# Keeping a convolution block's scan inputs and gate in PSUM, in place: scans of 512 columns, VectorE's stages split at their links, 28 places for expert states, new orders

## What is computed

```
x = x + L0_conv(ln(x)) ; x = x + L0_ffn(ln(x)) ; x = x + L1_conv(ln(x)) ; x = x + L1_ffn(ln(x))

conv:  inp, og, fg = split(z @ in_w + in_b, 3)
       inp, og, lam = silu(inp), sigmoid(og), sigmoid(fg)
       inp_f = (1 - lam)[..., d, None] * inp[..., None, e]        # per head 2 x 2, so 128 channels
       h_t = lam_t * h_{t-1} + inp_f_t     along rows and along columns, forward and reverse, summed
       out = sum_d state[..., d, e] * og[..., d];  layernorm * gamma + beta;  @ out_w + out_b
L0_ffn: 16 experts of 128, top 2 of softmax;  silu(z @ w1) * (z @ w2) @ w3, weighted
L1_ffn: 8 experts of 256, top 2;              gelu(z @ W1 + b1) @ W2 + b2, weighted
```

## Time and profile before

| | us |
|---|---|
| median of three runs (261.26 to 262.43) | 261.69 |
| the profiled execution | 262.96 |
| its span, first to last instruction | 261.1 |
| busy: PE / DVE / ACT / POOL | 217.1 / 219.8 / 166.8 / 162.6 |
| mean granted TensorE clock | 0.961 |

### The profile page before, as it was taken

One profiled execution on the slowest core, in us unless ns is written; L12 is line 12 of the kernel. 1 busy time (PEld: TensorE's weight loads), 2 busy tenths in 40 slices (PEclk: granted clock), 3 DMA queues, 4 the chain that ended last, 5 costly groups with the idle time before them and its releaser, 6 DMA issues.

```text
span 261.1 us, 3879 instructions
## 1 busy us (share of the span) xinstructions
PE 217.1 (83%) x1013; PEld 134.5 (52%) x1013; DVE 219.8 (84%) x591; ACT 166.8 (64%) x392; POOL 162.6 (62%) x182
## 2 busy tenths in 40 slices
PE   0843887698999797999799888779698998989992
PEld 0633854477676545665355446246445636465441
DVE  3988899999999899999999999999986979517033
ACT  3572887279447375546486547789679986684570
POOL 3565589658558642776738989657657787704232
PEclk9999999599799997799999999999799999999999
DMA  3790015855205900049100950000520070052621
GB/s 113 156 227 12 1 33 134 171 87 127 38 1 115 203 13 0 0 105 204 21 0 7 216 107 1 1 0 0 124 43 0 4 161 3 1 120 47 144 57 40
DMA packets 20210, 18.52 MB, mean 71 GB/s; under 512 B 5703, under 2 KB 15069, under 8 KB 20189
## 3 DMA queue, kind: packets, MB, share of 16 engines
q1 hardware_dynamic: 20168, 18.28, 33.9%
q10 hardware_dynamic: 20, 0.00, 0.0%
HBM read 17.56 MB, written 0.72 MB: 70 GB/s over the span
## 4 chain that ended last, share of the span: by engine, by line
PE 36%; DVE 31%; issue 14%; POOL 10%; ACT 7%; DMA 1%; POOLq 1%; DVEq 0%; ACTq 0%
PE bank L1059 12%; PE bank L1060 10%; PE bank L1166 8%; POOL total L619 5%; DVE hidden L1005 5%; PE bank L1063 4%; DVE weighted L1024 3%; DVE rev_h L942 2%; ACT hidden L782 2%; ACT norm_e L661 2%; DVE rows L967 1%; DVE rev_w L942 1%; DVE shift_a L893 1%; DVE fwd_h L941 1%; DVE best_at L990 1%
## 5 line engine op out<-in xcount | busy, mean ns | idle before, releaser
L1059 PE MATMUL bank<-tok_z,up_hi 128*128 128x512 f32 (+1 forms) x224 | 91.3, 414 | 6.6 <-DVE rows L967 1.4
L1060 PE MATMUL bank<-tok_z,up_lo 128*128 128x512 f32 (+1 forms) x224 | 84.4, 381 | 0.0
L619 POOL TENSOR_TENSOR total<-total,weighted 128x512 f32<-128x512 f32 (+1 forms) x47 | 58.5, 1245 | 22.0 <-DVE weighted L1027 12.3
L1166 PE MATMUL bank<-hidden,down 128*64 128x512 f32 (+1 forms) x288 | 64.2, 571 | 3.1 <-DVE hidden L1005 2.0
L1059 PEld LDWEIGHTS bank<-tok_z,up_hi 128*128 128x128 f32 x224 | 45.7, 204 | 31.1 <-issue 12.7
L773 ACT ACTIVATE silu_h<-bank 128x512 f32<-128x512 f32 (+1 forms) x80 | 40.2, 513 | 25.4 <-PE bank L1060 19.2
L1060 PEld LDWEIGHTS bank<-tok_z,up_lo 128*128 128x128 f32 x224 | 46.0, 205 | 5.4
L782 ACT ACTIVATE hidden<-bank,expert_bias 128x512 f32<-128x512 f32 x64 | 40.5, 689 | 8.6 <-PE bank L1060 8.4
L1005 DVE TENSOR_TENSOR hidden<-silu_h,bank 128x512 f32<-128x512 f32 (+1 forms) x80 | 42.8, 567 | 0.5 <-PE bank L1060 0.5
L1166 PEld LDWEIGHTS bank<-hidden,down 128*64 128x64 f32 x288 | 18.3, 141 | 36.1 <-issue 22.1
L1024 DVE TENSOR_TENSOR weighted<-bank,gates_b 128x512 f32<-128x512 f32 (+1 forms) x35 | 19.6, 574 | 0.4 <-POOL total L619 0.4
(11 more groups left out here) (126 smaller groups left out, 392.6 us busy)
## 6 DMA issues: line engine op xcount, KB each, us to landing
gates_b<-gates_dram SPq DMA_DIRECT2D x12, 512.0 KB, 6.3
gates_b<-gates_dram SPq DMA_DIRECT2D x6, 1024.0 KB, 9.8
up_raw<-in_L_ffn_w_dram SPq DMA_DIRECT2D x8, 192.0 KB, 4.5
up_raw<-in_L_ffn_W_dram SPq DMA_DIRECT2D x2, 512.0 KB, 6.3
up_raw<-in_L_ffn_w_dram SPq DMA_DIRECT2D x4, 128.0 KB, 2.8
down<-in_L_ffn_w_dram SPq DMA_DIRECT2D x1, 512.0 KB, 7.6
down<-in_L_ffn_W_dram SPq DMA_DIRECT2D x1, 512.0 KB, 7.8
out_dram<-rows SPq DMA_DIRECT2D x4, 128.0 KB, 4.1
```

Of the source, the lines that this page charges most:

```text
L619: nc.gpsimd.tensor_tensor(t, t, weighted[:, n % WEIGHTED, 0:c], ALU.add).then_inc(s_sum, 1)
L1059: nc.tensor.matmul(dst, hi, z, start=True, stop=False)
L1060: return nc.tensor.matmul(dst, lo, z, start=False, stop=True)
L1166: last = nc.tensor.matmul(t[k * D:(k + 1) * D, 0:c], w, hidden_of(first + k, j), start=(j == 0), stop=(j == l))
```

## The change

The scan inputs stay in PSUM. `vi` writes the silu back to bank `I`, where it came from; `aw` makes the row scans' input there in place, and `ca` writes the turned copy into bank `F`, which `tf` has read. `to` writes the gate's tanh back to bank `O`. `value_i`, `tanh_o`, `add_w` and `add_h` are gone. So the banks are freed later: `I` and `F` by the column scans (`sc`), `O` by `og`. In PE's string `vi`, `tf` and `to` are no longer names that free a bank.

With no padding a scan is over 512 columns, and the factor that cuts a sequence off is a zero in the factors: forward scans have it at a sequence's first position, reverse scans at its last, hence two sets of factors in each direction, `lam_fw`, `lam_rw`, `lam_fh`, `lam_rh`, of 15 out of 16 columns each, written by two ACT instructions in place of one. Both scan stages wait for `ca` (before, `sw` waited for `aw` alone).

DVE's functions are cut at their links into stages with names of their own (`a0 a1 a2`, `e0 e1 e2`, `lh lg ma pl mk`, `xh x`, `av aw`), so that other work can stand between. `NORM_BY_SCALAR` shrinks: the rows of units 5 to 8 are normalised by DVE. `HIDDENS` goes from 16 to 28, `WEIGHTED` from 2 to 3. All strings are new; SP's loads of layer 1's `in` and `down` weights come before the first gates. `BY_POOL` is empty, so the paths for it add no instruction.

```diff
-NORM_BY_SCALAR = {"a": (2, 3, 4, 5, 6, 7, 8), "e": (2, 3, 4, 5, 6, 7, 8)}
-SILUS, HIDDENS, WEIGHTED = 3, 16, 2
+NORM_BY_SCALAR = {"a": (2, 3, 4), "e": (2, 3, 4)}
+SILUS, HIDDENS, WEIGHTED, COPIES = 3, 28, 3, 2
...
 SP_ORDER = """
-gates up1 in1 gates gates gates gates gates gates gates gates store store store store
+in1 gates up1 gates gates gates gates gates gates gates gates store store store store
...
-        FREED = {"za": s_z["a"], "ze": s_z["e"], "tf": s_tanh_f, "vi": s_value, "to": s_tanh_o, "y": s_conv,
+        FREED = {"za": s_z["a"], "ze": s_z["e"], "sc": s_scan_h, "og": s_gated, "y": s_conv,
...
             def pads(_):
-                for t in (lam_w, lam_h, add_w, add_h):
-                    last = nc.gpsimd.memset(t[:, 0:SCAN:PAD], 0.0)
+                for t in (lam_fw, lam_fh):
+                    nc.gpsimd.memset(t[:, 0:TOK:SEQ], 0.0)
+                for t in (lam_rw, lam_rh):
+                    last = nc.gpsimd.memset(t[:, SEQ - 1:TOK:SEQ], 0.0)
...
             def value(u):
+                t = bank("I", u)[:, 0:c]
...
+                if u in ONE_SILU:
+                    nc.scalar.activation(t, t, ACT.Silu, bias=column(l, I_B)).then_inc(s_value, 1)
+                    return
...
+                nc.scalar.activation(tanh_i[:, 0:c], t, ACT.Tanh, bias=half_bias[:, I_B, l:l + 1], scale=0.5)
+                nc.scalar.activation(t, t, ACT.Identity, bias=column(l, I_B)).then_inc(s_value, 1)
...
+            def lambdas(t, u, n, ap):
+                return nc.scalar.activation(square(t, u)[:, :, :, n], ap[:, :, :, n], ACT.Copy, bias=0.5, scale=0.5)
...
-                nc.scalar.activation(by_image(body(lam_w, u), u), square(tanh_f, u), ACT.Copy, bias=0.5,
-                                     scale=0.5).then_inc(s_lam_w, 1)
+                lambdas(lam_fw, u, slice(1, SEQ), square(tanh_f, u))
+                lambdas(lam_rw, u, slice(0, SEQ - 1), square(tanh_f, u)).then_inc(s_lam_w, 1)
...
+                t = bank("O", u)[:, 0:c]
+                nc.scalar.activation(t, t, ACT.Tanh, bias=half_bias[:, O_B, l:l + 1], scale=0.5).then_inc(s_tanh_o, 1)
...
-                nc.scalar.activation(turned(body(add_h, u), u), by_image(body(add_w, u), u),
-                                     ACT.Copy).then_inc(s_add_h, 1)
+                nc.scalar.activation(turned(bank("F", u), u), square(bank("I", u), u), ACT.Copy).then_inc(s_add_h, 1)
...
+                lambdas(lam_fh, u, slice(1, SEQ), turned(tanh_f, u))
+                lambdas(lam_rh, u, slice(0, SEQ - 1), turned(tanh_f, u)).then_inc(s_lam_h, 1)
...
-                nc.vector.scalar_tensor_tensor(by_image(body(add_w, u), u), square(tanh_f, u), 1.0, square(value_i, u),
-                                               ALU.subtract, ALU.mult).then_inc(s_add_w, 1)
+                nc.vector.scalar_tensor_tensor(t, tanh_f[:, 0:c], 1.0, t, ALU.subtract, ALU.mult).then_inc(s_add_w, 1)
...
-                    dve.wait_ge(s_add, u + 1)
+                    c = columns_of(u)
+                    add = bank(src, u)
+                    dve.wait_ge(s_add_h, u + 1)
...
-                    nc.vector.tensor_tensor_scan(fwd[:, 0:end], lam[:, 0:end], add[:, 0:end], 0.0, ALU.mult, ALU.add)
-                    nc.vector.tensor_tensor_scan(rev[:, end:0:-1], lam[:, end:0:-1], add[:, end:0:-1],
+                    nc.vector.tensor_tensor_scan(fwd[:, 0:c], lam_f[:, 0:c], add[:, 0:c], 0.0, ALU.mult, ALU.add)
+                    nc.vector.tensor_tensor_scan(rev[:, c - 1::-1], lam_r[:, c - 1::-1], add[:, c - 1::-1],
                                                  0.0, ALU.mult, ALU.add).then_inc(s_scan, 1)
...
-                nc.vector.scalar_tensor_tensor(gated[:, 0:c], tanh_o[:, 0:c], 1.0, gated[:, 0:c],
+                nc.vector.scalar_tensor_tensor(gated[:, 0:c], bank("O", u)[:, 0:c], 1.0, gated[:, 0:c],
```

More of the change, by code:

```diff
@@ L8 @@
 SEQ = 16
-PAD = SEQ + 1
 IMAGE = H * W
@@ L12 @@
 TOK = 2 * IMAGE
-SCAN = 2 * SEQ * PAD + 1
 MOST = 2 * HALF
@@ L112 @@
 PAIR = [(u, q) for u in range(len(UNITS)) for q in range(EXPERTS[layer(u)] // 2)]
-STEPS_0 = sum(1 for u, _ in STEP if layer(u) == 0)
+STEPS_OF = [[n for n, (u, _) in enumerate(STEP) if layer(u) == l] for l in range(LAYERS)]
 def pairs_before(u):
@@ L150, in residents, with by_pool_before @@
     first, end = images(u)
-    return [v for v in range(SECOND) if images(v)[0] < end and images(v)[1] > first]
+    return [v for v in range(len(UNITS)) if layer(v) == 0 and images(v)[0] < end and images(v)[1] > first]
+def by_pool_before(n):
+    return sum(m < n for m in BY_POOL)
 def chunk(pair):
@@ L507, in store_rows @@
             def store_rows(v):
-                u = SECOND + v
+                u = [u for u in range(count) if layer(u)][v]
                 first, end = images(u)
@@ L514, in _ @@
             played(SP_ORDER, {"in1": second_in, "up1": second_up, "gates": broadcast_gates, "store": store_rows})
-            sp.wait_ge(s_out, 16 * (count - SECOND))
+            sp.wait_ge(s_out, 16 * sum(layer(u) for u in range(count)))
         @block.gpsimd
@@ new lines, in aggregate, with make, spreads @@
+            def aggregate(n):
+                def make(u):
+                    dve.wait_ge(s_stats[n], u + 1)
+                    for k in range(tiles_of(u)):
+                        last = nc.vector.bn_aggr(moments[n][:, k, :], stats[n][:, k, :])
+                    last.then_inc(s_moments[n], 1)
+                return make
+            def spreads(n, eps):
+                def make(u):
+                    t = tiles_of(u)
+                    dve.wait_ge(s_moments[n], u + 1)
+                    if u:
+                        dve.wait_ge(s_rstd[n], u)
+                    nc.vector.tensor_scalar(spread[n][:, 0:t], moments[n][:, 0:t, 1], eps, None,
+                                            ALU.add).then_inc(s_spread[n], 1)
+                return make
@@ L990, in choose, with marks @@
                     last = nc.vector.max_index(best_at[:, k, :], best[:, k, :], logits[:, k, 0:e])
-                link(last)
+                last.then_inc(s_found, 1)
+            def marks(u):
+                e, t = EXPERTS[layer(u)], tiles_of(u)
+                dve.wait_ge(s_found, u + 1)
                 if u:
```

326 lines of the change are left out of this document (175 added, 151 removed).

## The result

The changed kernel takes **243.73 us** (median of 4 runs, 242.28 to 244.6) beside 261.58 for the kernel before in the same rounds: a ratio of 0.9307, with a 95% interval from 0.9257 to 0.9358. That is 17.9 us less. The forecast was 254.5 in a range from 244 to 264: the sign was right, the size was not, and the time lies just under the range. The gain is more than twice the 7.2 us that were forecast.

What follows compares the result with a forecast made beforehand. DVE was taken to bound the kernel, lengthened by waits for POOL. DVE -13.0 (-21.1 + 9.3 - 1.2), banks +2.1 and tail +3.7 gave -7.2 us: 254.5 from a median of 261.69, range 244 to 264.

Steps and rivals of the forecast that it cites:

- What bounds the kernel: From 20 to 200 us DVE, busy 171.5 of 180 us, is what all other engines run behind.
- Scans, row inputs, gate, silu: DVE instructions reading a bank escape the wait for POOL: -12.4, -5.1, -2.7 and -0.9, together -21.1 us.
- the rival in which the bank doesn't end the wait: Wait due to SBUF factors or the output; scans give only 3.0 us: +10.9, 272.6 us; chance 0.04.
- Normalising, +9.3: Units 5 to 8 on DVE: 32 tiles add 15.3 us, eight small products save 6.0; between +4.0 and +14.7.
- Links, -1.2 (0 to -2.5): Work put between dependent DVE steps fills about half of some 2.5 us idle time behind links.
- Banks, +2.1: PE up steps while two or more banks hold a conv product: 45 more, at 0.047 us each.
- The rival that runs out of banks: PE stops for lack of banks held up by DVE's scans: slower, 263 to 270 us; chance 0.13.
- Places and the third buffer, nothing taken: A third `weighted` buffer and 28 places let PE and DVE run further apart; no time counted.
- Tail, +3.7: After the last logits PE has eight pairs of down products, not six; two pairs take 3.65 us.
- three signs of being wrong: Scans slower from a bank, DVE's normalising tiles hanging on POOL, or DVE below 90% busy between 20 and 190 us.
- all goes well, under 250: Normalising tiles at 0.312 us (+4.0), no price for banks, links filled: -15.9, 245.8 us; chance 0.20.
- nothing comes of it: PE waits on the chain through POOL, so DVE's saved 13 us become idle: about 261 us; chance 0.13.

Runs made afterwards that it cites:

- gates by pairs: Changed kernel with the last two units' gates broadcast in one 128 KB transfer per pair and half, not two of 512 KB: 239.44 us, ratio 0.914.

## Why the prediction was wrong

*What bounds the kernel.* Right for the kernel before (6.2 us of time for 7.3 off DVE). **The step that failed** is the one from DVE's time to the kernel's, "nearly each microsecond taken off it moves what follows", carried through to the end of the sum: after the change 12.4 us off DVE bring 1.0. The sum added gains and losses on DVE as if each were worth its duration on either side. Two of its terms show it, normalising and links.

*Scans, row inputs, gate, silu.* Forecast -21.1 on DVE. By the durations of both traces it was -12.0 (51.1 to 39.0), -4.9, -2.6 and -0.9, together -20.4. The mechanism and the prices were right, and the rival in which the bank doesn't end the wait is out. Not in the sum: other instructions with two inputs in SBUF got shorter too, the low parts by 4.2 us (`parts_e` from 0.83 to 0.53), which fits POOL's being busy 20.6 us less.

*Normalising, +9.3.* The largest loss of the sum, and **mis-sized**. 32 tiles added 14.5 us of durations (means of 0.41 and 0.51, within the bounds), and the small products gave back 9.5 where I had 6.0: +5.0 from trace to trace. Undone in the changed kernel it is 11.8 us of DVE's busy time. The price in time was nothing either way (243.4 with ACT, 243.7 with DVE); without it the forecast would have been 245.2.

*Links, -1.2 (0 to -2.5).* Wrong as a step, not only in size: I priced the idle time in front of a waiting step. DVE's busy time fell by 26.7 us, its durations by 20.3; the other 6.4 are overlap between neighbours, which the idle column can't show, and the `hidden` products between the steps keep PE going. Undone, the split costs 13.5 us, where the sum had 1.2.

*Banks, +2.1.* PE's waits for column scans, gate, `hidden` and `weighted` sum to 1.3 + 2.7 + 0.5 + 1.1 = 5.6, under the 7 that I had set as the sign of the forecast. In the kernel before the same waits of its products were 0 + 1.4 + 2.9 + 1.1 = 5.4, so that nearly nothing was added:

```profile
PE bank L1166 <- DVE hidden L1005: 2.0, 2, 1.4
PE bank L1121 <- DVE gated L958: 1.4, 1, 1.4
PE bank L1059 <- DVE weighted L1024: 1.1, 2, 0.7
PE bank L1059 <- DVE hidden L1005: 0.5, 3, 0.2
PE bank L1063 <- DVE hidden L1005: 0.4, 1, 0.4
```

The 5.3 that I spread over 112 steps are waits of PE's weight loads, another row. The rival that runs out of banks was not at work. The rule that stood with it, to empty a bank early, would have meant inputs in SBUF, and the run that reads all of them there is 23 us slower; since that run gives its banks back at the same times, what early emptying alone would bring was not run.

*Places and the third buffer, nothing taken.* Right for 28 against 24 (0.5 us), wrong below: with 20 it is 5.7.

*Tail, +3.7.* It was 5.9, and 2.7 with gates by pairs. The two more pairs are PE's work as I said; the rest was the gates' way through DRAM, which I saw in the stretch and did not price.

*Signs and rivals.* None of the three signs of being wrong came: scans from a bank are not slower, most normalised tiles take 0.31 us (single ones up to 1.5), and DVE is 93.7% busy from 20 to 190 us. A full DVE did not tell that the bound had moved. DVE's busy time (193.1, not 207) and the last logits (207.3, not 224) came out far better than I had set them. The time lies in the class "all goes well, under 250", which had 0.20, but only in part by its conditions: no price for banks came true, tiles at 0.312 did not, and the links gave more than it allowed. And the rival "nothing comes of it" was added up wrongly: -2.6 and +3.7 give 262.8, not 261.

*The numbers together.* With normalising and banks at nothing, the overlap at 6.4 and the tail at 5.9 the sum would have been 254.5 - 9.3 - 2.1 - 5.2 + 2.2 = 240.1, near the 243.7 measured. That is no proof, since the parts don't add: undone one at a time, the scans' inputs are worth 15.3, the other operands some 8, the split 13.5, together twice the gain. They hang on one another, as it seems because each piece taken out brings back waits of PE that the others had removed. Whether an order laid out anew for inputs in SBUF would lose less than 15 us was not tried and stays open.

## What to carry to other kernels

Where a DVE instruction with two inputs in SBUF has a spread that POOL's instructions explain, leave one input in the bank it was computed in, if the banks last. A sum of durations holds only as long as the same engine is the bound: cut its work in the old kernel and, as soon as it can be built, in the new one, and see what the time does. Splitting a chain of dependent steps pays only with work from an order laid out for it between the steps; a like split in another order cost as much as the whole change gave.
